# Context attention of a fused perceiver stack: keys turned over three units, copies between the parts of the exponentials, exponentials turned two groups at a time

## The chip, the core and the metric

One core of one Trainium2 chip runs the whole program as a single launch. The metric is the device time of that launch in microseconds (us), the median of repeated runs. TensorE (PE, with its weight loads as PEld) multiplies, ScalarE (ACT) takes exponentials and copies, VectorE (DVE) subtracts, reduces and scales, GpSimd (POOL) prepares operands, and the queue of SyncE (SP) issues the transfers.

## What is computed

The program is a perceiver of two layers: six stages A to F, each a layer norm, a mixer and a residual sum. The change touches only the second layer's cross attention, stage D. Its queries are 8 batches of 64 tokens and 16 heads, its context 1601 rows of 128 values for each batch. Cut to what matters:

```python
q_big = rope(einsum('bshk,hkq->bshq', hidden_q @ Wq.T, w_kc_q))
kv_r  = kv_c * cos_k + rotate_half(kv_c) * sin_k        # [8, 1601, 128]
scores = einsum('bhsr,bhlr->bhsl', einsum('bshq,hqr->bhsr', q_big, W_qr),
                einsum('bld,hdr->bhlr', kv_r, W_kr))
attn  = softmax(scores, axis=-1)
ctx_c = einsum('bhsl,bld->bhsd', attn, kv_r)            # then w_kc_kv and Wo
```

The kernel folds `W_kr` into the queries, so the rotated context `kv_r` is the key matrix and the value matrix at once.

## The kernel before

**Units.** The attention is cut into 32 units, four for each batch. Unit `8 * i + k` (an outer loop over `i`, `k` written out from 0 to 7) holds 256 query columns, 4 heads of 64 tokens, as two rows `r` of 128. Every product in float32 precision is made of three matmuls on high and low parts (`product`, L758 to L762): the high part is a rounded copy made by ScalarE or GpSimd, the low part a difference made by VectorE or GpSimd.

**Data.** `kv` is one buffer with the context of a batch, 13 tiles of 128 rows (the last has 65). SyncE loads it once `keys_t` says that all four key parts of the batch before are turned and once `values_split` says that the batch's value pair is made. GpSimd prepares it: four instructions rotate it in place (L618, L619, L623, L626), and two more (L632, L636) split it into `kv_pair` once the values of the batch before the last are all summed. TensorE turns `kv` to `kv_t` in four parts (`turn_keys`, L1144), each copied out of PSUM by ScalarE (`keys_in`, high part) and VectorE (`keys_in`, low part).

**A row's softmax.** TensorE makes the scores of a row in PSUM banks 0 to 3, 400 columns in each (`score_row`, L1154), each bank as soon as the exponentials of the row before have left it. VectorE takes the maximum in two halves (L2158) and negates it (L2165, `neg_m`). ScalarE then runs three exponentials with a sum each (`exps`, L1600): columns 0 to 799 out of banks 0 and 1 (L1604), and two of 400 columns out of banks 2 and 3 (L1609). VectorE makes the reciprocals of the row sums and two diagonal matrices of them (`row_scales`, L2177), which TensorE spreads over the partitions (L1191).

**A unit's values.** The exponentials lie with queries on the partitions, so TensorE turns them back in seven groups q = 0 to 6 of four transposes (the last has two), into banks 4, 5 and 7 in rotation (`turn_exp`, L1170). ScalarE copies a group to `expo_t` (L1616), VectorE writes its low part (L1795, the line that all low parts share), and TensorE adds it to the sum in bank 6 (`add_values`, L1180, six matmuls for a group). The sum goes out by ScalarE (`out_c`, L1650) and VectorE (`big`, L2217). A bank of the rotation is written again only once the low part of its last content is made.

**Order.** Each engine runs an order written out by hand (`units`, one for each engine). In a unit k that turns no keys it is, with S1 for the scores of the second row of unit k + 1, S0 for those of the first row of unit k + 2, D for the diagonals, V0 to V6 for the value groups, T3 to T6 for turning this unit's exponentials and A0 to A2 for turning the first three groups of the next:

```
TensorE  S1 D V0 T3 V1 T4 V2 T5 V3 T6 S0 V4 A0 V5 A1 V6 A2
ScalarE  queries, copy 3, exps of S1 (3 parts), copies 4 5 6, copy A0, exps of S0 (3 parts), out, copies A1 A2
VectorE  low A2, maxima of S1, low 3, low of queries, lows 4 5 6, maxima of S0, low A0, row_scales, out, low A1
```

The keys of the next batch are turned in unit k = 1 and in unit k = 5: there each of T3 to T6 is followed by one key part, so eight groups share the three banks.

## Time and profile before

| | us |
|---|---|
| median of 3 runs | 1669.83 |
| lowest and highest of them | 1669.3, 1681.73 |
| the profiled execution | 1675.27 |
| its span, first to last instruction | 1673.4 |
| TensorE busy in the span | 1476.4 |
| VectorE busy in the span | 1144.1 |
| ScalarE busy in the span | 633.6 |
| GpSimd busy in the span | 723.2 |
| attention stage, 698.35 to 1149.50 us of the span | 451.15 |

The time of a run holds some 2 us around the span. Busy times are unions of the instructions' spans in the profile, and neighbouring instructions of one engine overlap by up to 0.1 us (on TensorE by more, since matmuls are pipelined and the ends are modelled), so the text counts from start to start. A wait's releaser is inferred from semaphore events.

### The profile page before, as it was taken

The numbers are of one execution on the slowest core, as the hardware profiler recorded it, in microseconds if no ns is written. First come the engines' busy times: TensorE is split into PE (matmuls) and PEld (weight loads), VectorE is DVE, ScalarE is ACT, GpSimd is POOL, SyncE is SP. The second block draws the span as 40 slices with busy tenths as digits, with TensorE's granted clock in tenths as the row PEclk, the third lists the DMA queues.
The fourth block names the chain that finished last, engine by engine and source line by source line (L and its number), as shares of the span: only waits on it lengthen the run. The fifth ranks groups of instructions, "written<-read, shape, count | busy, mean of one in ns | idle before, by whom it ended". The sixth has DMA issues, their size and how long they took to land.

```text
span 1673.4 us, 23622 instructions
## 1 busy us (share of the span) xinstructions
PE 1476.4 (88%) x8264; PEld 1195.2 (71%) x8264; DVE 1144.1 (68%) x1625; ACT 633.6 (38%) x1294; POOL 723.2 (43%) x484
## 2 busy tenths in 40 slices
PE   6777799989979999789988998998967877889998
PEld 3555558857857777688988988997755666656886
DVE  3539446656666888588888788775469999652564
ACT  2322333342332333456655655664233333322000
POOL 2234237745846666323233132202635555342664
PEclk9798879988998999899999999999978888998999
DMA  3111113322332222000000000001311111111322
GB/s 124 39 38 64 26 38 90 94 63 64 93 113 76 90 88 60 21 21 22 1 20 21 21 0 30 17 1 34 104 32 52 42 39 50 38 63 40 99 88 76
DMA packets 31027, 87.62 MB, mean 52 GB/s; under 512 B 3424, under 2 KB 3552, under 8 KB 30560
## 3 DMA queue, kind: packets, MB, share of 16 engines
q1 hardware_dynamic: 30944, 86.56, 16.4%
q8 instruction: 47, 0.77, 0.2%
q14 instruction: 36, 0.29, 0.1%
HBM read 85.50 MB, written 1.05 MB: 52 GB/s over the span
## 4 chain that ended last, share of the span: by engine, by line
PE 62%; DVE 20%; ACT 9%; issue 7%; DVEq 1%; DMA 1%; ACTq 0%; SPq 0%
PE psum L760 18%; PE psum L762 17%; PE psum L761 17%; DVE part_max L2158 5%; ACT expo L1609 3%; DVE expo_t L1795 2%; ACT expo L1604 2%; PE psum L987 1%; PE psum L793 1%; DVE diag L2177 1%; PE psum L1321 1%; ACT expo_t L1616 1%; DVE q_pair L1795 1%; PE psum L789 1%; DVE conv_acc L2282 1%
## 5 line engine op out<-in xcount | busy, mean ns | idle before, releaser
L606 POOL TENSOR_SCALAR wpair<-landing 128x1024 fp32r<-128x1024 f32 (+3 forms) x120 | 115.5, 963 | 448.5 <-PE psum L762 353.1
L609 POOL TENSOR_TENSOR wpair<-landing,wpair 128x1024 fp32r<-128x1024 f32 (+3 forms) x120 | 254.7, 2123 | 10.0
L760 PE MATMUL psum<-xn,wpair 128*128 128x512 f32 x508 | 214.7, 423 | 24.3 <-DVE xn L1795 19.6
L762 PE MATMUL psum<-xn,wpair 128*128 128x512 f32 x508 | 209.5, 412 | 0.0
L761 PE MATMUL psum<-xn,wpair 128*128 128x512 f32 x508 | 209.3, 412 | 0.0
L1616 ACT CAST expo_t<-psum 128x512 fp32r<-128x512 f32 (+1 forms) x224 | 117.2, 571 | 154.6 <-PE psum L1177 154.6
L1795 DVE TENSOR_TENSOR expo_t<-psum,expo_t 128x512 fp32r<-128x512 f32 (+1 forms) x224 | 138.2, 647 | 49.2 <-ACT expo_t L1616 48.0
L760 PEld LDWEIGHTS psum<-xn,wpair 128*128 128x128 f32 x508 | 101.6, 200 | 59.6 <-issue 19.6
L760 PE MATMUL psum<-expo_t,kv_pair 128*128 128x256 f32 (+1 forms) x416 | 137.2, 330 | 1.5 <-DVE expo_t L1795 1.5
L1177 PE MATMUL psum<-const,expo 128*128 128x128 f32 (+1 forms) x832 | 128.2, 274 | 9.8 <-DVE kv_t L1795 9.8
L2158 DVE TENSOR_REDUCE part_max<-psum 128x1 f32<-128x804 f32 x128 | 122.2, 985 | 11.4 <-PE psum L762 9.7
L663 POOL TENSOR_TENSOR wpair<-landing,wpair 128x512 fp32r<-128x512 f32 x80 | 120.4, 1505 | 6.7
L762 PEld LDWEIGHTS psum<-xn,wpair 128*128 128x128 f32 x508 | 100.7, 198 | 25.3
L761 PEld LDWEIGHTS psum<-xn,wpair 128*128 128x128 f32 x508 | 101.9, 201 | 23.3
L762 PE MATMUL psum<-expo_t,kv_pair 128*128 128x256 f32 (+1 forms) x416 | 116.9, 281 | 0.0
L761 PE MATMUL psum<-expo_t,kv_pair 128*128 128x256 f32 (+1 forms) x416 | 116.8, 281 | 0.0
L760 PE MATMUL psum<-kv_t,q_pair 128*128 128x402 f32 x256 | 96.2, 376 | 22.9 <-DVE q_pair L1795 14.8
L660 POOL TENSOR_SCALAR wpair<-landing 128x512 fp32r<-128x512 f32 x80 | 54.5, 681 | 127.7 <-issue 106.6
L1177 PEld LDWEIGHTS psum<-const,expo 128*128 128x128 f32 (+1 forms) x832 | 97.6, 141 | 11.5 <-DVE kv_t L1795 11.3
L761 PE MATMUL psum<-kv_t,q_pair 128*128 128x402 f32 x256 | 90.6, 354 | 0.0
L762 PE MATMUL psum<-kv_t,q_pair 128*128 128x402 f32 x256 | 90.4, 353 | 0.0
L618 POOL TENSOR_TENSOR kv_turn<-kv,rope_k 128x832 f32<-128x832 f32 x8 | 15.8, 1975 | 162.0 <-DMA kv<-in_ctx 162.0
(301 smaller groups left out, 3607.9 us busy)
## 6 DMA issues: line engine op xcount, KB each, us to landing
landing<-in_weights SPq DMA_DIRECT2D x71, 512.0 KB, 3.5
landing<-in_weights SPq DMA_DIRECT2D x97, 256.0 KB, 2.6
kv<-in_ctx SPq DMA_DIRECT2D x8, 832.0 KB, 4.4
landing<-in_weights SPq DMA_DIRECT2D x16, 384.0 KB, 3.0
landing<-in_weights SPq DMA_DIRECT2D x15, 320.0 KB, 2.9
rope_k<-in_rope_k SPq DMA_DIRECT2D x1, 1664.0 KB, 6.7
const<-in_constants SPq DMA_DIRECT2D x1, 1216.0 KB, 7.5
x<-in_x SPq DMA_DIRECT2D x1, 1024.0 KB, 5.0
```

The lines of the kernel that those rows point to most:

```text
L606: pool.tensor_scalar(wpair[:, slot, 0, 0:width], landing[:, slot, 0:width], 1.0, 1.0, ALU.mult, ALU.mult).then_inc(chunk_high, 1)
L609: pool.tensor_tensor(wpair[:, slot, 1, 0:width], landing[:, slot, 0:width], wpair[:, slot, 0, 0:width].bitcast(F32), ALU.subtract).then_in ...
L660: pool.tensor_scalar(quarter_part(q, 0), quarter(landing, q), 1.0, 1.0, ALU.mult, ALU.mult).then_inc(chunk_high, 1)
L663: pool.tensor_tensor(quarter_part(q, 1), quarter(landing, q), quarter_part(q, 0).bitcast(F32), ALU.subtract).then_inc(chunk_split, 1)
L760: pe.matmul(out, w(0), act(0), start=start, stop=False)
L761: pe.matmul(out, w(0), act(1), start=False, stop=False)
L762: return pe.matmul(out, w(1), act(0), start=False, stop=stop)
L1177: mm = pe.transpose(bank(k_bank)[0:rows, at:at + P], expo[:, k % 2, r, t * P:t * P + rows], constant("ident"))
L1609: act.activation(expo[:, buffer, r, at:at + width], bank(c)[:, 0:width], ACT.Exp, bias=neg_m[:, r:r + 1], accum_out=part_sum[:, buffer, r, ...
L1616: act.copy(expo_t[0:rows, q % 4, 0, 0:width], bank(k_bank)[0:rows, 0:width]).then_inc(exp_t_high, 1)
L1795: return dve.tensor_tensor(out, value, high.bitcast(F32), ALU.subtract)
L2158: dve.tensor_reduce(part_max[:, r, half:half + 1], psum[:, 2 * half:2 * half + 2, 0:402], mybir.AxisListType.XY, ALU.max).then_inc(max_par ...
```

## The change

`turned_batch` now gives a batch for three units in a row, k = 0, 1, 2 and again k = 4, 5, 6. The 13 key tiles are parted 4, 4, 1 and 4 instead of 4, 4, 4 and 1: part 0 is turned in the first of the three units (after T3), parts 1 and 2 in the second (after T3 and T4), part 3 in the third (before T3). On TensorE the groups T3 to T6, with keys among them, are turned at two places instead of four, after V1 and after V3, and A0 is moved behind V5, to A1. On ScalarE the three exponentials of a row no longer run as one block: those of S1 stand behind the first three copies, one by one; those of S0 behind copy A0, behind copy A1 and behind the copy out. On VectorE low A1 moves ahead of the output's multiplication. In a unit without keys:

```
TensorE  S1 D V0 V1 T3 T4 V2 V3 T5 T6 S0 V4 V5 A0 A1 V6 A2
ScalarE  queries, copy 3, exp a, copy 4, exp b, copy 5, exp c, copy 6, copy A0, exp a, copy A1, exp b, out, exp c, copy A2
```

The number of instructions, their sizes and their engines stay, but for the widths of two key copies and their low parts.

```diff
@@ -732,7 +732,14 @@
 
         def turned_batch(i, k, last):
 
-            return {1: 2 * i + 1, 5: None if last else 2 * i + 2}.get(k)
+            return 2 * i + 1 if k < 3 else 2 * i + 2 if k in (4, 5, 6) and not last else None
+
+        KEY_TILES = ((0, 4), (4, 8), (8, 9), (9, KT))
+
+        def key_columns(part):
+
+            first, end = KEY_TILES[part]
+            return first * P, min(end * P, CTX) - first * P
 
         TURN_BANKS = (4, 5, 7)
 
@@ -741,7 +748,9 @@
 
             order = [("exps", q) for q in range(3, 7)]
             if turned_batch(0, k, last) is not None:
-                order = [g for part, exps in enumerate(order) for g in (exps, ("keys", part))]
+                order = ([*order[:1], ("keys", 0), *order[1:]],
+                         [*order[:1], ("keys", 1), order[1], ("keys", 2), *order[2:]],
+                         [("keys", 3), *order])[k % 4]
             before = [("exps", q) for q in range(3)] + order
             return [(*g, TURN_BANKS[n % 3], before[n]) for n, g in enumerate(order)]
 
@@ -1144,9 +1153,9 @@
 
                     if part == 0:
                         pe.wait_ge(kv_step, 3 * b + 3)
-                    for k in range(4 * part, min(4 * part + 4, KT)):
+                    for k in range(*KEY_TILES[part]):
                         rows = P if k < KT - 1 else LASTK
-                        at = (k - 4 * part) * P
+                        at = (k - KEY_TILES[part][0]) * P
                         mm = pe.transpose(bank(k_bank)[:, at:at + rows], kv[0:rows, k, :],
                                           constant("ident", rows)[:, 0:rows])
                     mm.then_inc(keys_t, 1)
@@ -1204,11 +1213,13 @@
                 def units(i, last):
                     for k in range(8):
                         unit, batch = 8 * i + k, turned_batch(i, k, last)
-                        groups = iter(context_groups(k, last))
-
-                        def turn():
-
-                            for _ in range(1 if batch is None else 2):
+                        groups = context_groups(k, last)
+                        per_values = {4: (0, 2, 0, 2), 5: (0, 3, 0, 2), 6: (0, 3, 0, 3)}[len(groups)]
+                        groups = iter(groups)
+
+                        def turn(count):
+
+                            for _ in range(count):
                                 kind, q, k_bank, (before, n) = next(groups)
 
                                 if before == "keys":
@@ -1224,8 +1235,6 @@
 
                             if q == 0:
                                 pe.wait_ge(exp_t_low, 7 * unit + 7)
-                            elif batch is not None:
-                                pe.wait_ge(keys_low, 4 * batch + 5 - q)
                             if k < 7:
                                 turn_exp(i, k + 1, q, TURN_BANKS[q])
                             elif not last:
@@ -1237,14 +1246,15 @@
                             score_row(i + 1, 0, 1)
                         for q in range(4):
                             add_values(i, k, q)
-                            turn()
+                            turn(per_values[q])
                         if k < 6:
                             score_row(i, k + 2, 0)
                         elif not last:
                             score_row(i + 1, k - 6, 0)
                         for q in range(3):
                             add_values(i, k, 4 + q)
-                            turn_ahead(q)
+                            for ahead in ((), (0, 1), (2,))[q]:
+                                turn_ahead(ahead)
 
                 pe.wait_ge(q_lat_in, XH + 1)
                 for part in range(4):
...
@@ -1597,17 +1607,18 @@
 
                     act.copy(q_pair[:, k % 2, 0, :], big[:, bass.ds(256 * (8 * i + k), 256)]).then_inc(qu_high, 1)
 
-                def exps(i, k, r):
-
-                    act.wait_ge(max_done, 2 * (8 * i + k) + r + 1)
+                def exps(i, k, r, step):
+
                     buffer = k % 2
-                    act.activation(expo[:, buffer, r, 0:800].rearrange("p (c n) -> p c n", c=2),
-                                   psum[:, 0:2, 0:400], ACT.Exp, bias=neg_m[:, r:r + 1],
-                                   accum_out=part_sum[:, buffer, r, 0:1]).then_inc(exp_done, 1)
-                    for c in (2, 3):
-                        at, width = ROW_CHUNKS[c]
-                        act.activation(expo[:, buffer, r, at:at + width], bank(c)[:, 0:width], ACT.Exp,
-                                       bias=neg_m[:, r:r + 1], accum_out=part_sum[:, buffer, r, c - 1:c]
+                    if step == 0:
+                        act.wait_ge(max_done, 2 * (8 * i + k) + r + 1)
+                        act.activation(expo[:, buffer, r, 0:800].rearrange("p (c n) -> p c n", c=2),
+                                       psum[:, 0:2, 0:400], ACT.Exp, bias=neg_m[:, r:r + 1],
+                                       accum_out=part_sum[:, buffer, r, 0:1]).then_inc(exp_done, 1)
+                    else:
+                        at, width = ROW_CHUNKS[step + 1]
+                        act.activation(expo[:, buffer, r, at:at + width], bank(step + 1)[:, 0:width], ACT.Exp,
+                                       bias=neg_m[:, r:r + 1], accum_out=part_sum[:, buffer, r, step:step + 1]
                                        ).then_inc(exp_done, 1)
 
                 def exp_t_in(i, k, q, k_bank):
...
@@ -1633,24 +1646,25 @@
                             unit_queries(i, k + 2)
                         elif not last:
                             unit_queries(i + 1, k - 6)
-                        turned_in(1)
-                        if k < 7:
-                            exps(i, k + 1, 1)
-                        elif not last:
-                            exps(i + 1, 0, 1)
-                        turned_in(3 if batch is None else 7)
+                        second_row = (i, k + 1, 1) if k < 7 else None if last else (i + 1, 0, 1)
+                        first_row = (i, k + 2, 0) if k < 6 else None if last else (i + 1, k - 6, 0)
                         after = (i, k + 1) if k < 7 else None if last else (i + 1, 0)
-                        if after is not None:
-                            exp_t_in(*after, 0, TURN_BANKS[0])
-                        if k < 6:
-                            exps(i, k + 2, 0)
-                        elif not last:
-                            exps(i + 1, k - 6, 0)
+                        for step in range(3):
+                            turned_in(1)
+                            if second_row is not None:
+                                exps(*second_row, step)
+                        turned_in(count - 3)
+                        for step in range(2):
+                            if after is not None:
+                                exp_t_in(*after, step, TURN_BANKS[step])
+                            if first_row is not None:
+                                exps(*first_row, step)
                         act.wait_ge(context_sum, 8 * i + k + 1)
                         act.copy(out_c[:, :], bank(6)[:, 0:256]).then_inc(context_in, 1)
+                        if first_row is not None:
+                            exps(*first_row, 2)
                         if after is not None:
-                            for q in (1, 2):
-                                exp_t_in(*after, q, TURN_BANKS[q])
+                            exp_t_in(*after, 2, TURN_BANKS[2])
 
                 act.sem_inc(exp_done, 3)
                 act.wait_ge(q_lat_in, XH + 1)
...
@@ -2206,18 +2223,17 @@
                         turned_in(1)
                         if first_row is not None:
                             unit_queries(*first_row)
-                        turned_in(3 if batch is None else 7)
+                        turned_in(count - 1)
                         if first_row is not None:
                             half_max(*first_row, 0, 0)
                             row_max(*first_row, 0)
                         if second_row is not None:
                             exp_t_in(*second_row, 0, TURN_BANKS[0])
                             row_scales(*second_row)
+                            exp_t_in(*second_row, 1, TURN_BANKS[1])
                         dve.wait_ge(context_in, unit + 1)
                         dve.tensor_tensor(big[:, bass.ds(256 * unit, 256)], out_c[:, :], bank(6)[:, 256:512],
                                           ALU.mult).then_inc(context_done, 1)
-                        if second_row is not None:
-                            exp_t_in(*second_row, 1, TURN_BANKS[1])
 
                 dve.sem_inc(context_done, 1)
                 for k in range(2):
```

## Rows read from the trace of the kernel before

**Rows 1.** Windows: A:B, length, busy us (count) of PE PEld DVE ACT POOL, clock, DMA, GB/s.

```profile
698.35:758.95 60.60, 55.36 (x377) 53.51 (x377) 46.77 (x80) 34.88 (x90) 13.69 (x6) 0.94 0.05 15
758.95:1049.49 290.54, 262.67 (x1887) 252.95 (x1886) 240.81 (x406) 174.53 (x446) 83.82 (x31) 1.00 0.05 17
1049.49:1103.29 53.80, 52.16 (x378) 50.65 (x377) 41.89 (x82) 34.95 (x90) 8.39 (x6) 1.00 0.05 13
1103.29:1149.50 46.21, 43.20 (x317) 41.53 (x316) 31.06 (x63) 27.31 (x68) 0.00 (x0) 1.00 0.01 1
```

**Rows 2.** Windows, three single units: plain, keys turned, context prepared.

```profile
862.80:875.30 12.50, 12.50 (x95) 12.32 (x93) 9.68 (x20) 8.19 (x22) 0.15 (x1) 1.00 0.00 0
829.60:845.80 16.20, 14.55 (x104) 13.72 (x104) 11.86 (x25) 10.26 (x28) 0.27 (x1) 1.00 0.15 53
845.80:862.80 17.00, 12.89 (x95) 12.30 (x93) 16.14 (x20) 8.21 (x22) 11.08 (x4) 1.00 0.00 0
```

**Rows 3.** Timeline (start, length) of TensorE, second half of a plain unit.

```profile
872.84 0.60 PE L1177 MATMUL psum<-const,expo 128*128 128x128 f32 x4
873.20 0.37 PE L760 MATMUL psum<-expo_t,kv_pair 128*128 128x256 f32 x1
...
874.00 0.60 PE L1177 MATMUL psum<-const,expo 128*128 128x128 f32 x4
...
875.29 0.45 PE L760 MATMUL psum<-kv_t,q_pair 128*128 128x402 f32 x1
```

**Rows 4.** Timeline of ScalarE, around two copies and the exponentials.

```profile
844.17 0.59 ACT L1616 CAST expo_t<-psum 128x512 fp32r<-128x512 f32 x1 [3.12 <-PE psum L1177]
844.65 0.93 ACT L1604 ACTIVATE expo<-psum,neg_m 128x800 f32<-128x800 f32 x1
...
873.48 0.59 ACT L1616 CAST expo_t<-psum 128x512 fp32r<-128x512 f32 x1 [2.19 <-PE psum L1177]
874.22 0.93 ACT L1604 ACTIVATE expo<-psum,neg_m 128x800 f32<-128x800 f32 x1
...
875.13 0.59 ACT L1609 ACTIVATE expo<-psum,neg_m 128x400 f32<-128x400 f32 x1
...
876.27 0.38 ACT L1650 COPY out_c<-psum 128x256 f32<-128x256 f32 x1
```

**Rows 5.** Timeline of VectorE: low parts, and diagonals written beside GpSimd.

```profile
837.54 0.69 DVE L1795 TENSOR_TENSOR kv_t<-psum,kv_t 128x512 fp32r<-128x512 f32 x1 [1.75 <-ACT kv_t L1590]
...
844.78 0.69 DVE L1795 TENSOR_TENSOR expo_t<-psum,expo_t 128x512 fp32r<-128x512 f32 x1 [0.58 <-ACT expo_t L1616]
...
845.78 3.72 DVE L2177 TENSOR_SCALAR diag<-const,sums 128x128 f32<-128x128 f32 x2
...
875.13 1.88 DVE L2177 TENSOR_SCALAR diag<-const,sums 128x128 f32<-128x128 f32 x2
```

**Rows 6.** Timeline of GpSimd: preparing one context, then splitting it.

```profile
845.53 1.98 POOL L618 TENSOR_TENSOR kv_turn<-kv,rope_k 128x832 f32<-128x832 f32 x1 [23.19 <-DMA kv<-in_ctx]
847.47 1.95 POOL L619 TENSOR_TENSOR kv_turn<-kv,rope_k 128x832 f32<-128x832 f32 x1
849.49 3.74 POOL L623 TENSOR_TENSOR kv<-kv,rope_k 128x1664 f32<-128x1664 f32 x1
853.31 3.73 POOL L626 TENSOR_TENSOR kv<-kv,kv_turn 128x1664 f32<-128x1664 f32 x1
...
875.15 1.59 POOL L632 TENSOR_SCALAR kv_pair<-kv 128x1664 fp32r<-128x1664 f32 x1 [18.11 <-PE psum L762]
876.83 3.80 POOL L636 TENSOR_TENSOR kv_pair<-kv,kv_pair 128x1664 fp32r<-128x1664 f32 x1
```

**Rows 7.** Timeline of TensorE, where keys are turned and after GpSimd ran.

```profile
838.29 0.33 PE L1177 MATMUL psum<-const,expo 128*128 128x128 f32 x1 [1.41 <-DVE kv_t L1795]
...
840.35 0.28 PE L1150 MATMUL psum<-const,kv 65*128 65x65 f32 x1
...
857.45 0.45 PE L760 MATMUL psum<-kv_t,q_pair 128*128 128x402 f32 x1 [2.41 <-DVE q_pair L1795]
```

More of the change, by code:

```diff
@@ L1588, in keys_in @@
                     act.wait_ge(keys_t, 4 * b + part + 1)
-                    at, width = 512 * part, min(512, CTX - 512 * part)
+                    at, width = key_columns(part)
                     act.copy(kv_t[:, buffer, 0, at:at + width], bank(k_bank)[:, 0:width]).then_inc(keys_high, 1)
@@ L1621, in units @@
                         batch = turned_batch(i, k, last)
-                        groups = iter(context_groups(k, last))
+                        groups = context_groups(k, last)
+                        count = len(groups)
+                        groups = iter(groups)
                         def turned_in(count):
@@ L1661, in _ @@
                 for unit, r in ((0, 0), (0, 1), (1, 0)):
-                    exps(0, unit, r)
+                    for step in range(3):
+                        exps(0, unit, r, step)
                 for q in range(3):
@@ L2139, in keys_in @@
                     dve.wait_ge(keys_high, 5 * b + part + (1 if part < 3 else 2))
-                    at, width = 512 * part, min(512, CTX - 512 * part)
+                    at, width = key_columns(part)
                     ins = low(kv_t[:, buffer, 1, at:at + width], bank(k_bank)[:, 0:width],
@@ L2188, in units @@
                         unit, batch = 8 * i + k, turned_batch(i, k, last)
-                        groups = iter(context_groups(k, last))
+                        groups = context_groups(k, last)
+                        count = len(groups)
+                        groups = iter(groups)
                         def turned_in(count):
```

## The prediction

> **What bounds the kernel now.** The page gives TensorE 88% of the span, a mean over stages with different limits. The change touches only the attention of stage D, so I took windows of that stage first, then single units in the timelines of TensorE, ScalarE and VectorE, and at last GpSimd. The stage is 451.15 us: four units with the start, 20 units in 290.54 us (five batches of 58.11), four units in 53.80 and the last four in 46.21 [rows 1]. The last two groups hold no rotation of a context (L618 to L626), the last no keys either. A plain unit takes 12.5 us, and TensorE is busy for all of it [rows 2]: here TensorE sets the pace, and whatever makes it wait is paid in full, 32 times. The two others cost more. The unit that turns keys takes 16.2 us, with 1.65 without work on TensorE (at 838.29 it waited 1.41 us for the keys' low part [rows 7]). The next one, beside which GpSimd rotates the next context, takes 17.0 us, with 4.1 us without work [rows 2]. So a batch of 58.1 is four plain units (50.2), some 3.5 for keys (1.5 of it transposes, the rest waits) and 4.4 beside GpSimd.
>
> Those 4.4 us come from VectorE. Its two diagonals took 3.72 us beside GpSimd's instructions [rows 5, 6], and the low part of the queries held the scores back by 2.41 us [rows 7]; in plain units a diagonal takes 0.2 to 0.3 us. Each such VectorE instruction, with its inputs in SBUF, ended when a GpSimd instruction did. Between L618 and L619 there is no gap, and the second diagonal waited for L619 too; between L632 and L636 lie 0.09 us, and there both diagonals slipped through (1.88 us in all, of which 1.59 is L632) [rows 5, 6].
>
> **Grouping on TensorE: nothing.** A group of four transposes is worth 0.36 us start to start, a value group behind it 0.80 [rows 3]. A value group behind another saves 0.08 (it starts without the 0.20 step behind transposes), but a transpose behind a transpose steps by 0.11 (0.60 for four, 0.27 of it the last one's own length), where the step to a value matmul is 0.03. So two groups are 0.79, two value groups 1.52, together 2.31 as before. The gap-free unit stays at some 12.4 us.
>
> **First new wait: V3 behind T3.** V3 needs group 3 turned, copied and its low part made. From the start of T3 the copy starts after 0.64 (872.84 to 873.48), takes 0.59, the low part follows 0.02 later (844.76 to 844.78) and takes 0.69, TensorE 0.06 later (838.23 to 838.29) [rows 3, 4, 5, 7]: 2.00 us. Before, TensorE had V1, T4, V2, T5 in between, 2.7 us. Now it has T3, T4 and V2, 0.79 + 0.80 = 1.59: a gap of 0.41, and 0.08 more since V3 starts cold. Nothing queued ahead makes it worse: by the same prices the maximum of S1 is done at 5.0 us of the unit, the low part starts at 5.6.
>
> **Second new wait: S1 behind A0.** The scores of the next row need banks 0 and 1, so the first exponential of the row before, which ScalarE runs behind copy A0. From A0 on: 0.64 to the copy, 0.48 to the exponential (844.17 to 844.65), 1.07 to the scores (874.22 to 875.29) [rows 3, 4]: 2.19 us. Before, TensorE had A0, V5, A1, V6 (three matmuls, 0.44) and A2 there, 0.36 + 0.80 + 0.36 + 0.44 + 0.36 = 2.3, and the scores came 2.45 after A0: just enough. Now V5 lies ahead of A0 and leaves 1.59: a gap of 0.60. The maximum is not what is late (done some 0.9 us before that exponential can start).
>
> **Third: the last exponential behind the copy out.** Exponentials take 0.91, 0.57 and 0.57 [rows 4]. With copy A1 (0.48) and the copy out (0.26) between them, the third leaves bank 3 some 0.14 us after the scores reach it; with the cold start 0.23.
>
> Sum for a plain unit: 12.37 + 0.41 + 0.08 + 0.60 + 0.23 = 13.7 us against 12.5 to 12.6, 1.13 more. Bounds: nothing, should all three be hidden; 1.5, should each hand-over cost 0.1 more.
>
> **Units with keys.** They start from 13.7, since the waits are the same. First unit: part 0 (0.44) fills V3's gap, but T6 waits for its bank: counted from T3, the first exponential leaves ScalarE at 0.64 + 0.48 + 0.91 = 2.03, copy and low part of part 0 end at 3.35; the scores start at 3.64 instead of 3.37. 13.95. Second: T5 waits for part 1 (3.40), T6 for group 4, which stands on ScalarE behind two exponentials and a key copy (copy to 3.68, low part to 4.40): scores at 4.69, 15.0. Third: part 3 comes before group 3 on ScalarE with two copies (0.56), then the first exponential (0.91), so copy 3 ends at 2.71, V3 starts at 3.48, scores at 4.85: 15.2. A batch is 13.7 + 13.95 + 15.0 + 15.2 = 57.8 us, 4.0 over today's 53.8 without GpSimd [rows 1]. The 1.4 us wait of today goes, but three units pay for it.
>
> **Beside GpSimd: 3.2 us back.** The transfer waits for the last key part, which now stands in the third unit. From the end of that transpose (840.63) to L618 (845.53) it is 4.9 us, from there to the end of L623 7.70 [rows 6, 7]. In the third unit part 3 ends at 5.0, so the rotation runs from 9.9 to 17.6 (end of L623) and 21.4. The diagonals of that unit come at 15.2 (A0 at 15.2 - 2.2 = 13.0, then 0.64 + 0.59 + 0.02 to its low part, 0.6 for it, 0.4 for the sums), inside L623, which ends at 17.6; both pass in the 0.08 us before L626 [rows 6], as they did at 876.74. Low A1 (0.6) and the output (0.4) follow, so D can start at 18.9 instead of 17.7: 1.2 us. The low part of the queries stands at 22.6, clear of L626. So 1.2 instead of 4.4. The range of this term is 0 (the diagonals fall into another gap) to 4.9 (the second diagonal waits for L626 too, 3.73 more). The split of `kv_pair` delays the diagonals as today and nothing behind them. GpSimd is in time: it is done 20 us before the next part 0 is turned.
>
> In the trace the diagonals end when GpSimd's instruction does, and what decides is the gap behind it (none behind L618, 0.09 us behind L632) [rows 5, 6]. The Trainium skill states it as a lock (SBUF — State Buffer, Who interferes with whom): whichever of the two starts first keeps the shared pair of ports for its whole instruction, and the other blocks fully. By that rule a diagonal that gets in before L626 delays GpSimd, which costs nothing here, and the sum stays at 1.2; if L626 gets in between the two, it is 4.9. No row has a diagonal between L623 and L626.
>
> **The sum.** A batch with rotation 57.8 + 1.2 = 59.0 against 58.1. First block 60.60: 59.0 and the same 1.3 of start, -0.3. Five batches at +0.9: +4.5. The batch with keys alone, 57.8 against 53.8: +4.0. The last four units: two at 1.13, 0.4 each for the two without new scores: +3.0. Together +11.2 us, on a profiled execution of 1675.27 (span 1673.4), which lies 5.4 above the median of 1669.83. Against that median: 1681 us. TensorE's granted clock is 1.00 even in the unit with 4.1 us of gaps [rows 2], so I give the new gaps no cost in clock.
>
> **Rivals.**
>
> 1. *The waits vanish.* The finer order on ScalarE might let every copy come early enough. Then a plain unit stays at 12.5, keys cost their transposes (1.5), GpSimd 1.2: 52.7 a batch, and the batch without GpSimd 51.5 against 53.8: 1669.8 - 6 x 5.4 - 2.3 = 1635. For it: ScalarE is busy for only 8.19 of 12.50 us, VectorE 9.68 [rows 2], so neither is full. Against: the two gaps are latencies of one chain, not work; idle engines don't shorten them.
> 2. *Both diagonals are caught*, or the rotation meets VectorE elsewhere, as today: 3.7 more in each of six batches, 1681 + 22 = 1703. For it: this is what happened between L618 and L619. Against: the 0.09 us gap at L632 let both through.
> 3. *The waits are there but smaller*, half of 0.41 and 0.60, say, because a copy's end and its successor overlap: -0.5 in each unit, 1665, no change.
> 4. *The change does nothing*: new waits and the relief cancel, 1670. By the prices above that needs half of the waits too, so it is one with 3.
>
> **How the numbers follow.** Less than 1% (16.7 us) is about what a measurement of this kernel can't tell from no change. My forecast 0.58, its own range 1673 to 1691; rival 1 0.10; rival 2 0.17; rivals 3 and 4 0.15. Slower by over 1% (from 1686.5) is rival 2 and a quarter of the forecast: 0.31. Faster is rival 1 (under 1653): 0.10. The rest, 0.59, is the same. The range leaves out rival 1 and the top of rival 2: 1661 to 1704.
>
> **What would show it.** Plain units of 13.6 to 13.8 us from S1 to S1; in each a gap of 0.4 on TensorE ahead of V3, released by the low part of `expo_t`, and one of 0.6 ahead of S1, released by L1604's successor line; VectorE's wait for `kv_t` short; the rotation one unit later, and beside it diagonals of about 2.6 us but no long low part of the queries. A plain unit of 12.5 would prove the two latencies wrong; gaps over 3 us at the diagonals would be rival 2. Wrong too would be the sum if T5 and T6 did not wait in the second key unit: then 1.3 us a batch, 9 us in all, go.

## The result and the profile after

| | before | after |
|---|---|---|
| median of 17 runs, us | 1670.46 | 1684.97 |
| the profiled execution, its span, us | 1675.27, 1673.4 | 1683.93, 1682.1 |
| TensorE busy in the span, us | 1476.4 | 1486.1 |
| VectorE, ScalarE, GpSimd busy, us | 1144.1, 633.6, 723.2 | 1125.6, 629.8, 726.2 |
| attention stage, us | 451.15 | 463.42 |

The forecast was 1681 us, with a range of 1673 to 1691; measured are 1684.97. The ratio of after to before, taken over the means of the 17 runs (1685.7 and 1672.8 us), is 1.0077, with a 95% interval from 1.0062 to 1.0093: 0.8% slower, or 12.9 us. The medians lie 14.5 us apart, the two profiled executions 8.7. The stage, from the first score of its first unit (693.59) to the end of its last output (1157.01), is 12.3 us longer. Line numbers of the kernel after are higher: scores and values are L769 to L771, transposes L1186, copies L1627, exponentials L1615 and L1620, low parts L1810, diagonals L2192 and L1200, the copy out L1663.

The windows of the kernel after, cut as those of before in [rows 1] (a window, its length, busy time and count of PE, PEld, DVE, ACT, POOL, then clock, DMA share, GB/s):

```profile
693.59:752.53 58.94, 54.27 (x377) 50.52 (x377) 43.14 (x79) 34.63 (x90) 14.32 (x6) 1.00 0.05 16
752.53:1047.75 295.22, 272.38 (x1886) 252.05 (x1886) 221.24 (x406) 171.79 (x446) 84.31 (x31) 1.00 0.05 16
1047.75:1105.57 57.82, 54.18 (x378) 50.40 (x378) 42.39 (x82) 34.31 (x90) 7.90 (x6) 1.00 0.04 12
1105.57:1157.01 51.44, 46.16 (x316) 42.94 (x316) 32.19 (x64) 26.98 (x68) 0.00 (x0) 0.97 0.00 1
```

A batch with a rotation is 59.04 us (295.22 over five), against 58.11; the batch with keys alone 57.82 against 53.80; the last four units 51.44 against 46.21. The waits of the whole stage name what holds TensorE (engine and line, releaser: us in all, times, longest):

```profile
PEld psum L769 <- ACT expo L1615: 18.0, 30, 0.6
PEld psum L769 <- DVE expo_t L1810: 15.8, 19, 1.4
PE psum L769 <- DVE expo_t L1810: 11.9, 19, 1.2
PEld psum L769 <- ACT expo L1620: 10.0, 30, 0.3
PE psum L1200 <- DVE big L2235: 7.4, 7, 2.0
PEld psum L1186 <- DVE kv_t L1810: 5.6, 14, 0.6
```

Thirty times the scores waited 0.6 us for the first exponential of the row before (L1615), and thirty times some 0.3 us for a later one (L1620). The value groups waited for the low part of `expo_t` 19 times (in a batch's first two key units key transposes fill that time). Before, a plain unit had nothing of this [rows 2].

Here is where the first two waits stand in one unit, the fourth of a batch. TensorE (start, length, operation, idle time before it and its releaser):

```profile
861.27 1.04 PE L1186 MATMUL psum<-const,expo 128*128 128x128 f32 x8
...
863.27 0.39 PE L769 MATMUL psum<-expo_t,kv_pair 128*128 128x256 f32 x1 [0.25 <-DVE expo_t L1810]
864.09 0.82 PE L1186 MATMUL psum<-const,expo 128*128 128x128 f32 x6
...
868.40 1.04 PE L1186 MATMUL psum<-const,expo 128*128 128x128 f32 x8
...
869.63 0.60 PE L1186 MATMUL psum<-const,expo 128*128 128x128 f32 x4
870.59 0.45 PE L769 MATMUL psum<-kv_t,q_pair 128*128 128x402 f32 x1 [0.36 <-ACT expo L1615]
```

The eight transposes of T3 and T4 start at 861.27, V2 follows, and V3 starts at 863.27: 2.00 us behind T3, as its chain needs. The scores come at 870.59, 2.19 after A0 (868.40), where the work in between ends at 869.63 + 0.36 = 869.99. (The idle time that a row shows counts from the modelled end of the last matmul, so it is some 0.2 us less than the gap from start to start: 0.25 for 0.41, 0.36 for 0.60.) The same chain on ScalarE and VectorE:

```profile
861.91 0.59 ACT L1627 CAST expo_t<-psum 128x512 fp32r<-128x512 f32 x1 [3.65 <-PE psum L1186]
862.39 0.94 ACT L1615 ACTIVATE expo<-psum,neg_m 128x800 f32<-128x800 f32 x1
...
869.03 0.59 ACT L1627 CAST expo_t<-psum 128x512 fp32r<-128x512 f32 x1 [2.88 <-PE psum L1186]
869.52 0.93 ACT L1615 ACTIVATE expo<-psum,neg_m 128x800 f32<-128x800 f32 x1
...
871.48 0.39 ACT L1663 COPY out_c<-psum 128x256 f32<-128x256 f32 x1
871.73 0.64 ACT L1620 ACTIVATE expo<-psum,neg_m 128x401 f32<-128x401 f32 x1
```

```profile
862.53 0.69 DVE L1810 TENSOR_TENSOR expo_t<-psum,expo_t 128x512 fp32r<-128x512 f32 x1 [0.75 <-ACT expo_t L1627]
...
868.44 0.15 DVE L2180 TENSOR_REDUCE neg_m<-part_max 128x1 f32<-128x2 f32 x1
869.65 0.69 DVE L1810 TENSOR_TENSOR expo_t<-psum,expo_t 128x512 fp32r<-128x512 f32 x1 [1.06 <-ACT expo_t L1627]
```

Copy 3 starts 0.64 after T3, its low part at 862.53 ends at 863.22, V3 follows. The maximum is there at 868.59 (868.44 and 0.15), 0.9 us before the exponential (869.52) that stands behind copy A0, so the maximum isn't what the scores wait for. The third exponential of the row stands at 871.73, behind the copy out (871.48).

Beside GpSimd, at the end of the third unit of the next batch, first GpSimd, then VectorE:

```profile
909.40 1.99 POOL L618 TENSOR_TENSOR kv_turn<-kv,rope_k 128x832 f32<-128x832 f32 x1 [33.93 <-DMA kv<-in_ctx]
911.35 1.97 POOL L619 TENSOR_TENSOR kv_turn<-kv,rope_k 128x832 f32<-128x832 f32 x1
913.39 3.76 POOL L623 TENSOR_TENSOR kv<-kv,rope_k 128x1664 f32<-128x1664 f32 x1
917.23 3.79 POOL L626 TENSOR_TENSOR kv<-kv,kv_turn 128x1664 f32<-128x1664 f32 x1
```

```profile
914.76 2.67 DVE L2192 TENSOR_SCALAR diag<-const,sums 128x128 f32<-128x128 f32 x2
917.35 0.68 DVE L1810 TENSOR_TENSOR expo_t<-psum,expo_t 128x512 fp32r<-128x512 f32 x1
917.95 0.41 DVE L2235 TENSOR_TENSOR big<-out_c,psum 128x256 f32 x1
```

Both diagonals are done at 917.43, 0.28 us after L623 ended (917.15); before [rows 5] the pair had taken 3.72. L626 starts at 917.23 beside the second one. In the six units beside a rotation the pair took 2.36 to 2.67 us.

### The profile page after: what moved, and what is told of

It reads as the page before. It is cut to its first block, busy times and chain, and to the rows that moved or that the text cites. A ratio compares the mean times of both kernels' runs of the same rounds, so it can differ in the third digit from the quotient of the medians.

```text
span 1682.1 us, 23616 instructions
## 1 busy us (share of the span) xinstructions
PE 1486.1 (88%) x8264; PEld 1190.0 (71%) x8264; DVE 1125.6 (67%) x1625; ACT 629.8 (37%) x1294; POOL 726.2 (43%) x484
## 4 chain that ended last, share of the span: by engine, by line
PE 75%; DVE 11%; ACT 6%; issue 5%; DMA 0%; DVEq 0%; ACTq 0%; SPq 0%
PE psum L769 22%; PE psum L771 20%; PE psum L770 20%; PE psum L1186 3%; ACT expo L1615 2%; PE psum L996 1%; ACT expo_t L1627 1%; PE psum L802 1%; PE psum L1331 1%; DVE expo_t L1810 1%; DVE conv_acc L2298 1%; PE psum L798 1%; PE psum L1350 1%; PE psum L1200 1%; DVE mix L2367 1%
## 5 line engine op out<-in xcount | busy, mean ns | idle before, releaser
L769 PE MATMUL psum<-xn,wpair 128*128 128x512 f32 x508 | 212.4, 418 | 23.8 <-DVE xn L1810 14.0
L1810 DVE TENSOR_TENSOR expo_t<-psum,expo_t 128x512 fp32r<-128x512 f32 (+1 forms) x224 | 143.8, 651 | 104.8 <-ACT expo_t L1627 103.8
L771 PE MATMUL psum<-xn,wpair 128*128 128x512 f32 x508 | 208.2, 410 | 0.0
L1627 ACT CAST expo_t<-psum 128x512 fp32r<-128x512 f32 (+1 forms) x224 | 124.5, 566 | 175.6 <-PE psum L1186 175.5
L769 PE MATMUL psum<-expo_t,kv_pair 128*128 128x256 f32 (+1 forms) x416 | 132.1, 318 | 11.9 <-DVE expo_t L1810 11.9
L769 PEld LDWEIGHTS psum<-xn,wpair 128*128 128x128 f32 x508 | 100.6, 198 | 59.3 <-issue 19.6
L1186 PE MATMUL psum<-const,expo 128*128 128x128 f32 (+1 forms) x832 | 118.3, 276 | 5.2 <-DVE expo_t L1810 2.8
L771 PE MATMUL psum<-expo_t,kv_pair 128*128 128x256 f32 (+1 forms) x416 | 117.4, 282 | 0.0
L771 PEld LDWEIGHTS psum<-xn,wpair 128*128 128x128 f32 x508 | 99.8, 196 | 24.8
L770 PE MATMUL psum<-expo_t,kv_pair 128*128 128x256 f32 (+1 forms) x416 | 117.2, 282 | 0.0
L770 PEld LDWEIGHTS psum<-xn,wpair 128*128 128x128 f32 x508 | 100.4, 198 | 23.0
L769 PE MATMUL psum<-kv_t,q_pair 128*128 128x402 f32 x256 | 99.1, 387 | 18.8 <-ACT expo L1615 17.2
L1186 PEld LDWEIGHTS psum<-const,expo 128*128 128x128 f32 (+1 forms) x832 | 95.0, 142 | 10.2 <-DVE kv_t L1810 5.6
L769 PEld LDWEIGHTS psum<-expo_t,kv_pair 128*128 128x128 f32 (+1 forms) x416 | 78.7, 189 | 17.0 <-DVE expo_t L1810 15.8
L770 PE MATMUL psum<-kv_t,q_pair 128*128 128x402 f32 x256 | 89.9, 351 | 0.0
```

The source lines that it names most:

```text
L769: pe.matmul(out, w(0), act(0), start=start, stop=False)
L770: pe.matmul(out, w(0), act(1), start=False, stop=False)
L771: return pe.matmul(out, w(1), act(0), start=False, stop=stop)
L1186: mm = pe.transpose(bank(k_bank)[0:rows, at:at + P], expo[:, k % 2, r, t * P:t * P + rows], constant("ident"))
L1627: act.copy(expo_t[0:rows, q % 4, 0, 0:width], bank(k_bank)[0:rows, 0:width]).then_inc(exp_t_high, 1)
L1810: return dve.tensor_tensor(out, value, high.bitcast(F32), ALU.subtract)
```

## The experiments

All are compared with the kernel before, run beside them on the same chip; the median of before in those sets was 1671.7 to 1672.5 us. The kernel after was measured in a set of its own (before: 1670.46), so a difference from its 1684.97 us is between sets. Times of a unit are from the start of S1 to the start of the next S1, read from the timeline of TensorE.

### The two hand-overs, undone one by one

**A0 back behind V4.** In `units` of TensorE:

```diff
-                            for ahead in ((), (0, 1), (2,))[q]:
+                            for ahead in ((0,), (1,), (2,))[q]:
```

> The changed kernel with one thing undone: TensorE turns A0 right behind V4 again, A1 behind V5, A2 behind V6; all else stays as changed. Theory (two hand-overs and one exponential set the plain unit): with A0 0.72 us earlier its copy and the first exponential are done when the scores come, so the 0.60 us gap ahead of S1 goes, and since the last exponential then ends earlier too, so do the 0.23 at the scores' fourth bank. Plain unit 13.75 to 12.9 us, 31 units times 0.85: 1685 to about 1659 us. Rival (the exponentials of a row, broken up by copies on ScalarE, are what costs): the order on TensorE doesn't matter, plain unit over 13.5, 1680 or more.

Measured: 1672.2 us, ratio 0.9992 (0.9975 to 1.0009). The plain unit is 13.05 us: 0.70 gone of the 0.85 expected; S1 no longer waits for the first exponential. The missing part is the third term: D still stands 2.47 us behind S1, not 2.31. But only 13 us came back, not 26. In the key units 0.3 to 0.7 us each came back, and in the units beside the rotation nothing (14.8 us), since with shorter units the diagonals met L623 nearer its start. VectorE and GpSimd in that kernel:

```profile
850.82 3.49 DVE L2192 TENSOR_SCALAR diag<-const,sums 128x128 f32<-128x128 f32 x2
854.23 0.68 DVE L1810 TENSOR_TENSOR expo_t<-psum,expo_t 128x512 fp32r<-128x512 f32 x1
```

```profile
850.27 3.76 POOL L623 TENSOR_TENSOR kv<-kv,rope_k 128x1664 f32<-128x1664 f32 x1
854.11 3.78 POOL L626 TENSOR_TENSOR kv<-kv,kv_turn 128x1664 f32<-128x1664 f32 x1
```

3.49 us for the two diagonals, against 2.67 in the kernel after, so D waited 1.9 us instead of 1.0. In this unit and in one more, 16.7 us long, TensorE's clock fell too (see below). The theory of the wait holds, the total was missed by what moved beside it.

**The turning places back.** In `units` of TensorE:

```diff
-                        per_values = {4: (0, 2, 0, 2), 5: (0, 3, 0, 2), 6: (0, 3, 0, 3)}[len(groups)]
+                        per_values = {4: (1, 1, 1, 1), 5: (2, 1, 1, 1), 6: (2, 1, 2, 1)}[len(groups)]
```

> The changed kernel with the other half undone: the groups 3 to 6 are turned one behind each of V0 to V3 again (in the units with keys two at the first place, and two at the third in the second key unit); A0 and A1 stay behind V5. Theory: V3 again has more than 2.0 us behind T3, so its 0.41 us gap and 0.08 of cold start go: plain unit 13.75 to 13.26, 32 times 0.49: about 1669 us. The gap ahead of S1 stays at 0.6. Rival (broken up exponentials): unchanged, 1680 or more.

Measured: 1669.06 us, ratio 0.9974 (0.9950 to 0.9998), plain unit 13.2 to 13.26. As expected, to 0.1 us.

**Both.**

> Both undone on TensorE; the keys over three units and ScalarE's and VectorE's new orders stay. Theory: plain unit 12.4 to 12.6 us as before the change; key units about 12.9, 14.0 and 13.7; beside GpSimd 1.2 at the diagonals. A batch of 54.3 against 58.1 before and 59.0 in the changed kernel: about 1646 us, faster than both. Rival (broken up exponentials cost): plain unit stays over 13, 1670 or more. Rival (spreading the keys gives nothing by itself, the time only moved with the grouping): 1668 to 1672, as before the change.

Measured: 1653.28 us, ratio 0.9876 (0.9860 to 0.9893). The plain unit is gap-free again, and the unit beside the rotation is the one that now costs most. A plain unit, the longest unit beside a rotation, and the batch without a rotation:

```profile
1085.43:1097.97 12.54, 12.54 (x95) 12.25 (x93) 9.89 (x20) 8.18 (x22) 0.00 (x0) 1.00 0.00 1
848.32:864.57 16.25, 14.30 (x95) 13.60 (x93) 12.93 (x20) 8.24 (x22) 6.99 (x2) 0.89 0.00 0
1032.10:1085.43 53.33, 52.16 (x381) 50.18 (x378) 43.12 (x82) 34.48 (x90) 8.59 (x6) 1.00 0.05 14
```

The undos nearly add up (13 and 16 us alone, 32 together), and the two rivals fall: with the interleaved exponentials and copies still in place, the plain unit is back at 12.5, and the kernel is clearly faster than before the change. Little of that comes from the keys themselves: the batch without a rotation takes 53.33 us against 53.80 in [rows 1]. A batch with one takes 55.1 to 55.5 us where the clock stays up, against 58.1; some 2.3 of these 2.8 us come from the later rotation, which holds VectorE up for less (14.3 to 14.7 us for the unit beside it, against 16.5 to 17.0). Key units were 13.4, 13.9 and 13.5 (expected 12.9, 14.0, 13.7). Most of the missing 7 us lie in the units beside the rotation, expected at 13.7: 14.3 to 14.7 us four times, 16.25 (above) and 15.99 once each, and for these two the clock is not 1.00 throughout (0.89 above); more on that below. (The profiled execution took 1658.54 us, 5 above the median of four.)

### The interleaving of ScalarE, undone

**ScalarE's old order** (the three exponentials of a row in one block, the copy out ahead of copies A1 and A2), TensorE's new one:

```diff
-                        for step in range(3):
-                            turned_in(1)
-                            if second_row is not None:
-                                exps(*second_row, step)
-                        turned_in(count - 3)
+                        turned_in(1)
+                        if second_row is not None:
+                            for step in range(3):
+                                exps(*second_row, step)
+                        turned_in(count - 1)
...
```

> The changed kernel with ScalarE's old order: the three exponentials of a row in one block, copies 4 to 6 behind them, the copy out ahead of copies A1 and A2. TensorE's new order stays. Theory: the two hand-overs stay, only the last exponential is early again: plain unit 13.75 to 13.5. The units with keys get worse, since a key copy or copy 3 stands behind 2.05 us of exponentials instead of 0.91: +1.1, +0.65 and +1.1 us. Together about 1698 us. Rival (broken up exponentials are what costs): plain unit back to 12.5, 1660 or less.

Measured: 1734.67 us, ratio 1.0351 (1.0327 to 1.0376). The direction is right, the size was far off: plain unit 14.29, not 13.5. I had left one edit of VectorE in place, low A1 ahead of the output's multiplication. With the copy out ahead of copy A1 it made the output wait for a copy that came later, and D for the output:

```profile
1160.62 0.45 PE L1200 MATMUL psum<-diag,const 128*128 128x256 f32 x1 [0.59 <-DVE big L2234]
```

So I restored that too.

```diff
                             exp_t_in(*second_row, 0, TURN_BANKS[0])
                             row_scales(*second_row)
-                            exp_t_in(*second_row, 1, TURN_BANKS[1])
...
+                        if second_row is not None:
+                            exp_t_in(*second_row, 1, TURN_BANKS[1])
```

> The changed kernel with ScalarE's old order (exponentials of a row in one block, the copy out ahead of copies A1 and A2) and with VectorE's old place for low A1, behind the output's multiplication. Theory: the kernel with ScalarE's order alone had plain units of 14.29 us, 0.8 more than I expected, since low A1 stood ahead of the multiplication and its copy behind the copy out, so the diagonals waited 0.6 us for the output. With the place restored that wait goes: plain unit 13.6, 1735 to about 1715 us. The two hand-over gaps (0.41 and 0.60) stay. Rival (one block of exponentials is slower by itself in this order): plain unit stays at 14.3.

Measured: 1700.71 us, ratio 1.0167 (1.0139 to 1.0196), plain unit 13.5. That is 14 us less than I had written down: the plain unit fell by 0.8, not 0.7, and the profile has five stretches of low clock in the stage where the one before had ten. The orders of the two engines belong together: 34 us lay in one low part. And the interleaving is worth 16 us in the changed kernel (1700.7 against 1685), all of it in units with keys, which take 14.9, 15.5 and 16.0 to 17.6 us here against 14.0, 15.0 and 15.1; the plain unit is 0.25 us longer with it.

**The third exponential ahead of the copy out**, all else as changed:

```diff
+                        if first_row is not None:
+                            exps(*first_row, 2)
                         act.wait_ge(context_sum, 8 * i + k + 1)
                         act.copy(out_c[:, :], bank(6)[:, 0:256]).then_inc(context_in, 1)
-                        if first_row is not None:
-                            exps(*first_row, 2)
```

> The changed kernel with the third exponential of the first row ahead of the copy out on ScalarE instead of behind it. Theory: the scores' fourth bank is free 0.26 us earlier, so the 0.23 us of the third term go: plain unit 13.75 to 13.5, 31 units: about 1678 us. Rival (that term is not on the path, the copy out is, since the diagonals wait for the output): no change or slower, 1685 to 1690.

Measured: 1682.16 us, ratio 1.0046 (1.0026 to 1.0067), plain unit 13.72. The scores no longer wait for the third exponential, but D now waits for the output, which comes 0.6 us later. The term is on the path, with the copy out right behind it: of 0.23 us, 0.03 came back. Here the rival was the better guide: the output is next on the path, though the measured time lies 3 us below what that rival gave.

### Spreading the keys alone

The kernel before with only the keys turned over three units: the first two undos, and both orders of ScalarE and VectorE as before.

> The kernel before the change with one part of the change alone: the keys turned over three units, with the new parting of tiles and the new places among the groups. The groups are turned one behind each value group, A0 behind V4, ScalarE runs a row's exponentials in one block, VectorE has its old order. Theory: plain units stay at 12.5; a key copy now stands behind 2.05 us of exponentials in each of three units, so these take about 14.0, 15.2 and 14.9 us; beside GpSimd some 0.6 instead of 4.4. A batch 57.2 against 58.1, the one without rotation 56.6 against 53.8: about 1668 us, the same as before. Rival (spreading the keys removes their wait whatever the copies do): key units 13.0 each, 1645 or less; then the interleaved copies are not what made the kernel with both undos fast.

Measured: 1679.92 us, ratio 1.0021 (0.9994 to 1.0048): no difference, though 12 us above my number. Plain units 12.5, key units 14.15, 15.17 (three of seven 16.72) and 16.32; beside the rotation 14.9 four times and 12.5 twice. The third key unit was to be 14.9. Its V3 waited as expected (1.79 us), and then TensorE ran slowly. Windows and the scores in that unit:

```profile
848.00:858.00 10.00, 8.21 (x63) 7.92 (x62) 7.17 (x17) 7.69 (x21) 0.23 (x1) 1.00 0.24 85
858.00:859.50 1.50, 1.50 (x8) 1.50 (x7) 0.60 (x2) 0.37 (x1) 1.50 (x1) 0.52 0.00 0
859.50:861.00 1.50, 1.50 (x6) 1.48 (x6) 0.42 (x1) 0.00 (x0) 1.50 (x2) 0.50 0.00 0
861.00:865.00 4.00, 4.00 (x31) 4.00 (x30) 2.90 (x5) 1.40 (x4) 3.92 (x2) 0.94 0.00 0
```

```profile
859.19 0.54 PE L770 MATMUL psum<-kv_t,q_pair 128*128 128x402 f32 x1
859.53 0.54 PE L771 MATMUL psum<-kv_t,q_pair 128*128 128x402 f32 x1
859.86 0.54 PE L769 MATMUL psum<-kv_t,q_pair 128*128 128x402 f32 x1
...
861.69 0.35 PE L769 MATMUL psum<-kv_t,q_pair 128*128 128x402 f32 x1
861.88 0.35 PE L770 MATMUL psum<-kv_t,q_pair 128*128 128x402 f32 x1
```

A granted clock of 0.50 is 1.2 GHz, half of the 2.4 GHz that 1.00 stands for: the scores came every 0.34 us instead of every 0.18. It lasted about 3 us. What it costs is read from the second key units: 16.72 us with such a stretch, 15.17 without, some 1.5 us. The profiled execution of this kernel has ten of them in the stage, that with ScalarE's old order ten as well, with VectorE's order restored five, those of the kernel before two (699.3 and 740.2), and that of the kernel after one, at its very end (1148.3). They change from one execution to the next: the ten runs of this kernel lie between 1668.7 and 1687.3 us, the profiled one is the slowest of them, and the fastest has the highest mean clock (0.939 against 0.929). The rival (13.0 us a key unit, whatever the copies do) falls: spread over three units without interleaved copies, the keys lose (58.15 us for the batch without a rotation, with one stretch of low clock, against 53.80), and the cheaper place of the rotation pays for it. Interleaved copies without spread keys were not run.

### The key parts at better places

The kernel with both undos, and the parts where the walk of the banks shows no wait:

```diff
-                         [*order[:1], ("keys", 1), order[1], ("keys", 2), *order[2:]],
-                         [("keys", 3), *order])[k % 4]
+                         [*order[:1], ("keys", 1), *order[1:3], ("keys", 2), *order[3:]],
+                         [*order[:1], ("keys", 3), *order[1:]])[k % 4]
...
-                        per_values = {4: (1, 1, 1, 1), 5: (2, 1, 1, 1), 6: (2, 1, 2, 1)}[len(groups)]
+                        per_values = {4: (1, 1, 1, 1), 5: (2, 1, 1, 1), 6: (2, 1, 1, 2)}[len(groups)]
...
+                        copies = (1, 1, 1) if count == 4 else (1, 2, 1)
                         for step in range(3):
-                            turned_in(1)
+                            turned_in(copies[step])
...
-                        turned_in(count - 3)
+                        turned_in(count - sum(copies))
```

> The kernel with both TensorE undos (1653 us) and the key parts placed so that no group waits for its bank: part 3 behind group 3 instead of ahead of it, part 2 behind group 5, and ScalarE copies a key part and the group behind it between the first and the second exponential. Theory: its key units took 13.4, 13.9 and 13.5 us; the second and the third fall to about 13.6 and 13.0: 0.8 us a batch, seven batches, about 1648 us. Rival (the extra time of a key unit is not the banks' wait but the transposes and VectorE): no change, 1653.

Measured: 1642.02 us, ratio 0.9811 (0.9783 to 0.9839). The second key unit is 13.38, the third 12.96, which is a plain unit and its four transposes. So the banks' wait was the cost of these units: 1.1 us a batch, about 8 us. The rest of the 11 us against the kernel with both undos lies in the units beside the rotation, which now take 13.6 to 13.9 us four times (16.1 and 14.5 twice), and that I had not forecast.

### GpSimd's instructions in pieces

Each of the six instructions for a context in five, for example:

```diff
-                pool.tensor_tensor(kv[:, :, :], kv[:, :, :], cos, ALU.mult).then_inc(kv_step, 1)
+                for a, z in pieces:    # (0, 3), (3, 6), (6, 9), (9, 12), (12, 13)
+                    ins = pool.tensor_tensor(kv[:, a:z, :], kv[:, a:z, :], cos[:, a:z, :], ALU.mult)
+                ins.then_inc(kv_step, 1)
```

In the kernel before:

> The kernel before the change, with each of GpSimd's six instructions for a context cut into five pieces of at most 384 of 1664 columns; nothing else differs. Theory (a VectorE instruction with its inputs in SBUF waits for the end of the GpSimd instruction that runs, and slips in behind it): the waits of 1.8, 2.0 and 3.75 us shrink to at most 0.9 each, the unit beside the rotation from 16.7 to about 14 us, six of them: 1670 to about 1654 us. Rival (GpSimd holds VectorE as long as it has work, or VectorE is slowed in proportion): no change or slower, 1670 to 1675.

Measured: 1645.23 us, ratio 0.9833 (0.9807 to 0.9859). The unit beside the rotation, 17.0 us in [rows 2], with GpSimd at work for nearly all of it:

```profile
832.84:845.32 12.48, 12.48 (x95) 12.31 (x93) 9.99 (x20) 8.17 (x22) 12.32 (x19) 1.00 0.00 0
```

```profile
832.78 0.85 DVE L2187 TENSOR_SCALAR diag<-const,sums 128x128 f32<-128x128 f32 x2
...
838.44 0.41 DVE L1805 TENSOR_TENSOR q_pair<-big,q_pair 128x256 fp32r<-128x256 f32 x1
```

The diagonals take 0.85 us, the low part of the queries 0.41 (3.75 before), beside the same work of GpSimd; in the six units like this one the pair takes 0.83 to 1.26. TensorE has no gap. The whole 4.4 us were the length of single instructions, and the kernel gains 26 us, six times 4.4, by a change that adds 190 instructions.

In the changed kernel:

> The changed kernel with each of GpSimd's six instructions for a context cut into five pieces, nothing else. Theory: in the changed kernel GpSimd costs only some 1.0 to 1.2 us in the fourth unit of a batch, so cutting its instructions brings the unit to 13.75 and 7 us in all: 1685 to 1678. It was 25 us in the kernel before the change. Rival (GpSimd still costs the changed kernel as much as before, and the longer units hide it): 1685 to 1665 or less.

Measured: 1680.75 us, ratio 1.0052 (1.0030 to 1.0074), 4.2 us less than the changed kernel's 1684.97, and its fourth units at 13.8 to 14.3 instead of 14.8 to 15.0. The intervals of the two ratios overlap, so the 4 us rest on the units of the profile, where the six beside a rotation are some 5 us shorter in all. GpSimd did cost the changed kernel little; the rival falls.

In the kernel with the key parts at better places:

> The kernel with the key parts behind group 3 and the same five pieces for each GpSimd instruction. Theory: what is left beside GpSimd (1.8 us at the diagonals of one unit, 0.4 at the split of the values) falls to 0.6 in all: 1.6 us in six batches, about 1638 us. Rival (as above): same as that kernel without the pieces, 1648.

Measured: 1629.43 us, ratio 0.9745 (0.9719 to 0.9771), 2.5% faster than before the change and 3.3% than after it, and 9 us below my number. Its five batches:

```profile
746.54:1005.65 259.11, 258.74 (x1889) 251.53 (x1887) 214.25 (x406) 172.04 (x446) 103.41 (x150) 1.00 0.06 19
```

51.8 us a batch, and TensorE idle for 0.4 of 259 us.

## Why the prediction was right

**The plain unit** was to be 13.7 us and is 13.74 to 13.76. V3 starts 2.00 us after T3 (863.27 and 861.27), S1 2.19 after A0: the two chains to the hundredth, since each link was read off a row of before. Undone one by one, the turning places took 0.5 us out of it and A0 0.7 (its 0.60 and 0.10 of the third term).

**The third term** (0.23 for the last exponential) is there: D stands 2.57 after S1 instead of 2.31. But taking it away gave 0.03. It was right as a term of the sum and wrong as a lever; I had not asked what is late next.

**Grouping on TensorE is worth next to nothing.** T3 and T4 together take 0.79 us (861.27 to 862.06), as forecast. A grouped kernel without waits was not run, but 13.76 less the waits (0.41 and 0.08, 0.60, 0.26) leaves 12.4, and ungrouped, with both undos, the plain unit is 12.50 to 12.54: 0.1 us.

**Units with keys** were to be 13.95, 15.0 and 15.2 and are 13.98, 15.03 and 15.1, by the waits that were named: in the second, T5 waits 0.3 us for the keys' low part and T6 0.4 for that of group 4, in the third V3 waits 1.21 us. The batch without rotation is 57.82 (57.8).

**Beside GpSimd** D was to wait 1.2 us; it stands at 3.49 to 3.79 behind S1 instead of 2.57, 0.9 to 1.2 us, and the batch is 59.04 (59.0). The diagonals met L623 and passed before L626, so the rival in which both are caught did not come. That the lock is one instruction long, which the Trainium skill states (SBUF — State Buffer, Who interferes with whom), is borne out by the pieces: the two diagonals shrank from 3.72 us to 0.85 with the same work beside them.

**The sum** was +11.2 us, and the stage grew by 12.3. The blocks: first 58.94 for 60.3 (-1.4), five batches +4.7 for +4.5, the next +4.0 for +4.0, the last four units +5.2 for +3.0. That the sum is off by 1.1 only is in part luck, since two errors offset each other:

- In the first block I kept 1.3 us of start. That start was a stretch of low clock at 699.3 (part of the 0.94 in [rows 1]), which the kernel after hasn't in its stage.
- The last two units, without new scores, were to cost 0.4 each and cost 2.9 together. This is the mis-sized term. The last unit's D waited 1.97 us, against 0.66 before, and TensorE fell to the low clock for about 3 us behind it. From the output before that D to the last output it is 10.18 us here, 9.09 with the same wait of 1.97 but no low clock (the third exponential ahead of the copy out), and 8.31 before. So of the 2.1 us missed 1.1 are the clock, and the rest waits that I didn't work out.

```profile
1146.97 0.45 PE L1200 MATMUL psum<-diag,const 128*128 128x256 f32 x1 [1.97 <-DVE big L2235]
```

The spans of the two profiled executions differ by 8.7 us and not by 12.3, because before the stage, where the kernels are the same, the one after is 4.8 us ahead, and behind it 1.2 us longer: such differences between executions are as large as the terms of the sum, and the forecast is better tested by the stage than by the medians.

**The clock** I gave no cost, from one unit with gaps of 4.1 us. For the kernel after that held but for the one stretch at its end. It is not a rule, and the trace of before could have told: of its six units beside a rotation, each with a wait of about 2.4 us ahead of the scores, the first had a stretch of low clock (740.2) and was 18.1 us long, the others 16.5 to 17.0. In the experiments with waits of about 1.8 us and more the clock fell many times. Ten stretches of some 1.5 us make 15 of the 19 us by which the profiled execution with the keys spread alone lies above my number, and 15 of the 37 us missed for ScalarE's old order.

The rival in which the waits vanish falls with the timeline, the one with half waits too: every link has its full length.

## What to carry to other kernels

Where one engine sets the pace without a gap, count for each consumer what that engine has to do between producer and consumer, and compare it with the chain through the others (here 2.0 us for turn, copy, low part; 2.2 for turn, copy, exponential): grouping work on the busy engine takes this cover away and saved at most 0.1 us there. Cut long GpSimd instructions that read SBUF beside a busy VectorE: the same work in five pieces each took 26 us off this kernel. And test the parts of a change alone: this one held a good part (copies between exponentials, keys over three units, and by the latter the rotation at a cheaper place) and a bad one, the grouping, and the bad one outweighed the good.

## What the runs showed of the hardware that I had not expected

- TensorE's granted clock fell to 0.50 for some 3 us behind waits of about 2 us, in some kernels ten times in the stage. Behind others as long it did not (2.4 us at 857.45 in [rows 7], at a clock of 1.00 in [rows 2]), not even at the same place of one kernel: with the keys spread alone, the second key unit waits 2.09 us at 840.74 and the clock falls, 2.03 us at 780.20 and it stays. What decides was not found out.
- A copy's low part on VectorE and an output queued in the wrong order cost 34 us (1734.7 against 1700.7), by 0.8 us in each plain unit (14.29 against 13.5; D waited 0.6) and by more low clocks behind the longer waits (ten stretches against five).
- Cutting GpSimd's instructions in fives lengthened L623 from 3.74 to at most 4.58 us, and the units beside that work take 12.5 to 12.6 us all the same.
